# A GRU and an attention block on one core: q and k of a third head moved into the recurrent stage

## Time and profile before

| | |
|---|---|
| median of 3 runs | 793.98 us (793.65 to 794.06) |
| profiled execution | 792.58 us, its span 790.8 us |
| recurrent stage, 17 to 276 us | granted TensorE clock 0.88 |
| last products of the stage to steady attention, 276 to 296 us | clock 1.00, TensorE busy 15.9 of 20 us |
| attention, 296 to 700 us | TensorE busy 394.5 of 404 us |
| feed-forward, from 700 us | 90.8 us |

### The profile page before, as it was taken

How to read it: one execution, slowest core, us unless ns; L and a number is a source line. 1 busy time by engine, 2 the same in 40 slices (tenths; PEclk the granted TensorE clock), 3 DMA queues, 4 the chain that set the end, 5 groups by cost and what they waited for, 6 DMA issues and landing times.

```text
span 790.8 us, 25165 instructions
## 1 busy us (share of the span) xinstructions
PE 736.6 (93%) x10368; PEld 534.4 (68%) x10368; DVE 585.9 (74%) x1582; ACT 479.2 (61%) x1613; POOL 105.3 (13%) x131
## 2 busy tenths in 40 slices
PE   6899898898989889999999999999989999999997
PEld 5787777787777666666666666666666666644545
DVE  4777777777777777777788887788877888744553
ACT  4444555445454567666677666776668776666453
POOL 0222222222222110000020010020010200100030
PEclk8878989889899999999999999999999999999999
DMA  6121112111121012222222323222222222210001
GB/s 224 43 97 42 44 45 81 43 43 43 46 74 36 3 25 38 48 40 43 42 42 41 42 41 42 41 41 41 42 41 41 41 41 42 41 28 27 19 10 53
DMA packets 77465, 36.70 MB, mean 46 GB/s; under 512 B 70395, under 2 KB 73639, under 8 KB 77223
## 3 DMA queue, kind: packets, MB, share of 16 engines
q1 hardware_dynamic: 76775, 33.52, 19.2%
q10 hardware_dynamic: 576, 1.57, 0.5%
HBM read 16.20 MB, written 2.10 MB: 23 GB/s over the span
## 4 chain that ended last, share of the span: by engine, by line
PE 74%; DVE 11%; ACT 9%; issue 3%; DMA 2%; DVEq 0%; SPq 0%; POOL 0%; ACTq 0%; POOLq 0%
PE bank L394 18%; PE bank L395 17%; PE bank L396 17%; PE bank L495 11%; PE bank L502 5%; DVE h_hi L1113 3%; PE bank L414 3%; ACT prob L914 3%; ACT zg L856 2%; ACT nu L859 2%; DVE prob L1210 1%; DVE aT_lo L1225 1%; DVE mx L1193 1%; DVE p_lo L1204 1%; ACT p_hi L907 1%
## 5 line engine op out<-in xcount | busy, mean ns | idle before, releaser
L394 PE MATMUL bank<-y_hi,w_hi 128*128 128x512 f16 (+1 forms) x412 | 136.8, 338 | 0.2 <-DVE qk_lo L1089 0.2
L495 PE MATMUL bank<-h_hi,whh_hi 128*128 128x16 f16 x1536 | 111.1, 175 | 27.6 <-DVE h_hi L1113 26.6
L395 PE MATMUL bank<-y_hi,w_lo 128*128 128x512 f16 (+1 forms) x412 | 136.2, 337 | 0.0
L396 PE MATMUL bank<-y_lo,w_hi 128*128 128x512 f16 (+1 forms) x412 | 136.1, 337 | 0.0
L495 PEld LDWEIGHTS bank<-h_hi,whh_hi 128*128 128x128 f16 x1536 | 91.5, 98 | 51.0 <-DVE h_hi L1113 50.0
L914 ACT ACTIVATE prob<-bank,nmx 128x128 f32<-128x128 f32 x256 | 90.4, 365 | 35.2 <-DVE nmx L1196 35.2
L495 PE MATMUL bank<-h_hi,whh_lo 128*128 128x16 f16 x1536 | 108.5, 173 | 0.0
L495 PEld LDWEIGHTS bank<-h_hi,whh_lo 128*128 128x128 f16 x1536 | 91.6, 98 | 0.3 <-issue 0.3
L395 PE MATMUL bank<-w_hi,y_lo 128*128 128x128 f16 x512 | 89.1, 219 | 0.0
L396 PE MATMUL bank<-w_lo,y_hi 128*128 128x128 f16 x512 | 89.1, 219 | 0.0
L394 PE MATMUL bank<-w_hi,y_hi 128*128 128x128 f16 x512 | 89.1, 219 | 0.0
(11 more groups left out here) (157 smaller groups left out, 2171.3 us busy)
## 6 DMA issues: line engine op xcount, KB each, us to landing
stage<-in_weights SPq DMA_DIRECT2D x16, 640.0 KB, 3.9
x<-in_x SPq DMA_DIRECT2D x16, 128.0 KB, 3.9
out<-xr SPq DMA_DIRECT2D x3, 512.0 KB, 3.1
w<-in_ada_r SPq DMA_DIRECT2D x1, 1024.0 KB, 7.1
pT_hi<-p_hi SPq DMA_TRANSPOSE x64, 2.4
pT_lo<-p_lo SPq DMA_TRANSPOSE x64, 2.5
w<-in_W_ih ACTq DMA_DIRECT2D x2, 384.0 KB, 3.7
w<-in_W_hh ACTq DMA_DIRECT2D x2, 384.0 KB, 6.7
```

The lines of the kernel that those rows point to most:

```text
L394: mm(ps, w[0], a[0], start=start, stop=False, skip_group_check=True)
L395: mm(ps, w[1], a[0], start=False, stop=False, skip_group_check=True)
L396: return mm(ps, w[0], a[1], start=False, stop=stop, skip_group_check=True)
L495: nc.tensor.matmul(out(m0 + m), half[:, k, w], h_hi[:, k * B:(k + 1) * B, 1], start=False, stop=False, skip_group_check=True)
```

## The change

`AHEAD` becomes `(0, 8, 14)`. Fillers of 128 columns in a block become: step 0 twelve and two transposes, step 1 three and the biases, step 2 twelve, step 3 twelve, step 4 ten, step 5 twelve and two transposes, step 6 six, step 7 five (and the modulation). All three heads are now made two blocks behind. The last two blocks of tokens of heads 8 and 14 are made at d = 0, with 256 columns a product, each head in a bank of its own (7 and 4), and rounded at d = 1 and d = 2. `rows_sum` is one operation after step 7. The row modulation of block 0 starts a step later. In the attention steps of heads made ahead `values` comes before `project_out`. The gate of the out-projection signals each of its two halves. `hf` shares memory with `nat0`, and the program asks for a smaller scratch for DMA descriptors.

```diff
-AHEAD = (0, 14)
+AHEAD = (0, 8, 14)
-ITEMS = NA * NBL
+ITEMS = [(e, n, 1) for n in range(NBL - 2) for e in range(NA)] + [(0, NBL - 2, 1), (0, NBL - 1, 1)]
+ITEMS += [(e, NBL - 2, 2) for e in range(1, NA)]
-ROW_TILES = {1: (0, 0), 2: (0, 1), 4: (1, 0), 5: (1, 1)}
-ADA_AT = 3
+ROW_TILES = {2: (0, 0), 3: (0, 1), 4: (1, 0), 5: (1, 1)}
+ADA_AT = 1
+AHEAD_PLACE = {0: (0, (0, 1)), 2: (1, (0,)), 3: (1, (1,)), 5: (2, (0, 1))}
+AHEAD_HIGH = {0: 0, 3: 1, 5: 2}
+AHEAD_LOW = {0: (0, (0,)), 1: (0, (1,)), 4: (1, (0, 1)), 6: (2, (0, 1))}
...
+        def ahead_place(item, part):
+            e, n, blocks = ITEMS[item]
+            ps, width = bank[4 if n < NBL - 2 else (4, 7, 4)[e] if (e, n) != (0, NBL - 1) else 6], blocks * BS * B
+            at = slice((4 - 2 * blocks) * P + part * width, (4 - 2 * blocks) * P + (part + 1) * width)
+            return ps[:, at].rearrange("p (b t) -> p b t", b=B), slice(n * BS, (n + blocks) * BS)
...
-            tall_at = {1: (0, 3), 2: (3, 4), 3: (4, 5), 4: (5, 8), 5: (8, 9), 6: (9, 12)}
+            tall_at = (0, 0, 4, 5, 6, 9, 9, 12)
-            share = (0, 0, 3, 8, 14, 25, 29, 34, 36)
-            share_0 = (0, 0, 0, 2, 11, 15, 19, 27, 36)
+            share = (0, 0, 3, 9, 15, 25, 25, 31, 36)
+            share_0 = (0, 0, 0, 0, 6, 11, 16, 26, 36)
...
-                    if s == 0 and r > 1:
-                        ahead(0, r - 2, 1)
-                    elif s in (2, 3) and r > 1 and NA > 1:
-                        ahead(1, r - 2, s - 2)
-                    elif s == 7 and r > 0:
+                    if r > 1 and s in AHEAD_PLACE:
...
+                        e, parts = AHEAD_PLACE[s]
+                        ahead(NA * (r - 2) + e, parts)
+                    elif s == 7 and r == NBL - 1:
+                        ahead(NA * (NBL - 2))
...
                 for k in range(KD):
+                    if g > 0 and head == 0:
+                        pe.wait_ge(o_gated, KD * (g - 1) + k + 1)
...
                 if d > WHOLE[0] and i not in AHEAD:
                     keys(d)
+                if i in AHEAD:
+                    values(d)
                 if d >= LAG and not late:
                     project_out(d - LAG)
-                values(d)
+                if i not in AHEAD:
+                    values(d)
...
-                    for part in range(2 * NA - 2):
-                        ahead(1, NBL - 1, part)
+                    for e in range(1, NA):
+                        ahead(ITEMS.index((e, NBL - 2, 2)))
...
-                if d == 1 and NA > 1:
-                    ahead_high(1, NBL - 1)
+                if 0 < d < NA:
+                    ahead_high(ITEMS.index((d, NBL - 2, 2)))
...
-                    elif s == 6:
-                        rows_sum(r, slice(0, 6))
-                    elif s == 7:
-                        rows_sum(r, slice(6, BS))
+                    if s == 7:
+                        rows_sum(r)
```

More of the change, by code:

```diff
@@ L175, in build @@
         adar = w32[:, 0:KD * 4 * D].rearrange("p (k c) -> p k c", k=KD)
+        hf = nat0[:, :, :].rearrange("p (a j) d -> p a (j d)", a=2)
         bT = small[:, 0:NB]
@@ L468, in tall_parts, with ahead @@
                 return mm
[L470 to L482 removed]
+            def ahead(item, parts=(0, 1)):
+                e = ITEMS[item][0]
+                for part in parts:
+                    ps, t = ahead_place(item, part)
+                    if part == 0:
+                        pe.wait_ge(lb_lo, t.stop // BS)
+                        if item > 0:
+                            pe.wait_ge(qk_l, min(item, ITEMS.index((0, NBL - 2, 1)) + 1))
+                    w = SLOTS.index((part, AHEAD[e]))
+                    for k in range(KD):
+                        mm = product(ps, (wq_hi[:, w, k, :], wq_lo[:, w, k, :]), (y_hi[:, k, :, t], y_lo[:, k, :, t]),
+                                     k == 0, k == KD - 1)
+                    if part == 1:
+                        mm.then_inc(qk_mm, 1)
             tall_rest = [(k, i) for k in range(KD) for i in range(3)]
[L485 removed]
+            tall_at = (0, 0, 4, 5, 6, 9, 9, 12)
             def gru_step(r, s):
@@ L560, in _ @@
                             pe.wait_ge(lb_lo, NBL - 2)
-                        for i in range(*tall_at[s]):
+                        for i in range(tall_at[s], tall_at[s + 1]):
                             tall_parts(tall_rest[i % 6:i % 6 + 1], i // 6, early)
-                    elif G1 <= r - ADA_AT < ADA and s == 6:
+                    elif G1 <= r - ADA_AT < ADA and s == 7:
                         if r - ADA_AT == G1:
@@ L568, in _ @@
             rows_T(NBL - 1)
-            ahead(0, NBL - 2, 1)
             pe.wait_ge(lb_lo, NBL - 1)
@@ L573, in _ @@
             rows_back(NBL - 1)
-            for part in range(2 * NA - 2):
-                ahead(1, NBL - 2, part)
-            for part in range(2):
-                ahead(0, NBL - 1, part)
+            ahead(ITEMS.index((0, NBL - 1, 1)))
             def norm_rows(g):
@@ L1279, in _ @@
                 value_low(d)
-                if d == 1 and NA > 1:
-                    ahead_low(1, NBL - 1)
+                if 0 < d < NA:
+                    ahead_low(ITEMS.index((d, NBL - 2, 2)))
                 if d > 1:
```

99 lines of the change are left out of this document (37 added, 62 removed).

## The result

The changed kernel takes 788.85 us (median of 5 runs, 787.46 to 790.42) against 793.65 us for the kernel before (5 runs, 791.79 to 794.06): ratio 0.9939, 95% interval 0.9925 to 0.9953, 4.8 us faster. The forecast was 783.4 us with a range from 778.5 to 788.5; the direction was right, the gain less than half of it, and the time lies 0.35 us outside the range.

What follows compares the result with a forecast made beforehand. TensorE was taken to bound attention, the ScalarE and VectorE chain the recurrent steps. Terms - 6.0 - 1.7 - 0.3 - 3.0 - 0.6 + 1.0 = - 10.6 from 793.98 gave 783.4 us, range 778.5 to 788.5.

Steps and rivals of the forecast that it cites:

- the price of values first: Attention, heads 0 and 14: values ahead of out-projection remove 8.1 us of aT_lo waits, landings and scatter take part: 1.7 won.
- the clock's 3.0 us: Recurrent stage: more filler in light steps 5 to 1 leaves about two clock falls in place of ten: 3.0 us won.
- Head 8 leaves the attention: Attention: each group loses 12 products, 2.59 us; late landings take part back; 1.5 us a group, 6.0 for four.
- The sign of being wrong that was named: Attention, head 8: gaps of over 1.5 us before attend would show the forecast wrong.
- the two edits with the gates: Attention: 6.0 us from head 8, 1.7 from values before out-projection, 0.3 from the gate that signals by halves.
- The full gaps don't overrun: Recurrent steps 0 and 5: 0.95 of 1.06 us filled, cost 0 at full clock; rival of overrun had chance 0.10.
- Block 0: Start of recurrent stage: modulation a step later avoids waiting for the adaln bias: 0.6 us won, bounds 1.4 won, 0.5 lost.
- Between the stages: Recurrent stage to attention: longer last sum, wider products at d = 0 and subtractions cost 1.0 us, bounds 0.4 and 2.6.
- attention is held by softmax and DMA: Rival, attention: late landings leave head 8 0.7 us a group, values first nothing: 788.3 us, chance 0.14.
- with five falls: Middle case of the rival that the recurrent stage's clock falls as often as now (793.3 us, chance 0.08): 786 us.
- the bound: Recurrent stage, worst case of the clock term: 7 us lost, from ten falls at 1.1 us against 4.2.
- The sum: Whole kernel: - 6.0 - 1.7 - 0.3 - 3.0 - 0.6 + 1.0 = - 10.6 us, giving 783.4 us.

Runs made afterwards that it cites:

- busier: Changed kernel with 9 products of 128 columns per block, from block 2 on, made twice for nothing: 787.89 us, ratio 0.9913 to the kernel before.

## Why the prediction was wrong, point by point

Two terms of the sum failed: the price of values first, and the clock's 3.0 us. The other points are smaller.

**Head 8 leaves the attention: the mechanism was right, the size about so.** Forecast -6.0. Measured as the difference between the kernels without head 8 (394.0, 394.1 and 394.3 us) and those with it (387.6): -6.5. TensorE's work went down by 10.8 us by the table (48 products of 0.216 us are 10.4) and its idle time up by 4 to 5. This holds with the values first in both; with the out-projection first in both it is 389.6 against 393.5 us, -3.9, and then the other order brings -2.0. The sign of being wrong that was named, a gap of over 1.5 us before `attend` at head 8, showed in one group of four (1.75 us).

**Values first: this step failed.** It said that the values take more than each wait for `aT_lo`, "so these go", and priced the landing that comes in their place. It did not ask what the values wait for. They write the bank that VectorE reads for `v_lo` of the head before, and moved forward they come to it 0.4 us early. The changed kernel at d = 14 (VectorE, TensorE, SyncE's queue), to be held against the earlier trace rows:

```profile
365.45 0.68 DVE L1199 TENSOR_TENSOR v_lo<-bank,v_hi 128x512 f16<-128x512 f32 x1
...
365.79 0.22 PE L403 MATMUL bank<-kT_lo,qT_hi 128*128 128x128 f16 x1
366.19 0.23 PE L401 MATMUL bank<-w_hi,y_hi 128*128 128x128 f16 x1 [0.18 <-DVE v_lo L1199]
...
368.62 0.38 PE L403 MATMUL bank<-aT_lo,w_hi 128*128 128x512 f16 x1
369.20 0.23 PE L401 MATMUL bank<-pT_hi,v_hi 128*128 128x128 f16 x1 [0.20 <-DMA pT_lo<-p_lo]
...
366.70 1.22 SPq L294 DMA_TRANSPOSE pT_lo<-p_lo  x1
```

That is 366.19 - 365.79 - 0.06 = 0.34 us here and at head 8, 0.6 us at head 0, and 4.6 us over eleven such heads. The waits for landings were priced at 11 x 1.1 = 12 us and are 8.6. Forecast for the two edits with the gates: -8.0; measured -5.9. The edit by itself, on the kernel before, gave nothing. The gate by halves was not undone alone; what it is worth stays open.

**The clock in the recurrent stage: the term of 3.0 us was mis-sized.** The direction was right: from 7 to 9 falls in blocks 2 to 13 to between 1 and 4, 2.9 in the mean. For these blocks I had 4.2 us lost before and 1.4 after, 2.8 won; measured against the same twelve blocks of 16.12 us it is 3.7 lost before and 3.2 after, 0.5 won. Of the 2.3 us that are missing:

- 0.5: the one profile lost 4.2, the mean of three is 3.7.
- 0.8: 2.9 falls at 0.75 us are 2.2 and not 1.4.
- 0.6: even a block without a fall takes 16.17 us and not 16.12. Step 1 is 2.02 us long, because VectorE waits in step 0 for ScalarE's rounding; with the sum of rows in two operations it is 1.98 again, so the six more products and the later sum make it together. The forecast had 0 here.
- 0.35: in block 13 VectorE stands still for 0.46 us before one `h_hi`, in all three profiles of the kernel before (step 4) and all nine of the changed code (step 3). I had counted it among the falls. Its cause the profiles don't show.

Blocks 14 and 15 gave 0.8 where I had 0.2: none of the nine has a fall there.

A fall before cost (197.1 - 193.4 - 0.35)/8 = 0.4 us, one now costs 0.75, though the clock was mostly low for 6.8 us then and for 3.4 us now. Two things differ. A fall now meets step 6 behind the twelve products of step 5. And the forecast took the block's one step of 2.25 us as fixed, which it is not: it is the step whose `h_hi` scan takes 0.56 us in place of 0.29, and in the kernel before it is missing in most blocks with a fall (it is there in 4, 6 and 7 of twelve blocks of the three profiles, in all twelve of the changed kernel). So a fall there came with 0.27 us less in the same block. In the first profile of each kernel ScalarE's rounding of a weight (`w_hi`) and GpSimd's `xb_lo` run beside each such scan; which of them makes it long was not tried, and 12 x 0.27 = 3.2 us lie there in the changed kernel. The clock of 0.95 was right and said little of the time: low clock is dear only where the gap is full.

**The full gaps don't overrun.** Steps behind twelve fillers are 1.98 us long, and with three products more still 2.00 (busier). So the row's 0.056 us per product was the price, and not the 81 ns that the Trainium skill gives for such a stream (TensorE: Matmul & The Clock Gate, Back-to-back issue gap): by that, fifteen products would take 1.2 us, an estimate from that page, in a gap of 1.06.

**Block 0: not measurable.** The stretch to block 2 scatters from 46.5 to 48.3 us over all profiles, and that hides the 0.6 us.

**Between the stages: +1.7 instead of +1.0.** The one profile before was the mild one of three. My term left the clock out: in all eleven profiles of this layout the clock fell there, so that the products from 279.55 on are 0.107 us apart where they had been 0.056. It fell in two of three profiles of the kernel before too, and in one of four with the gap filled. The fillers of block 14 that left are the likely reason, but the longest wait there grew only from 1.52 to 1.85 us (before 277.84), so that they are the reason is argued and not shown.

**The rival that came nearest** was "attention is held by softmax and DMA", at 788.3 us, to which I gave 0.14. Its place was right: taking the low half's landing away brings 6.0 us. Its reason, that head 8 itself wouldn't pay, was wrong, and that its time lies 0.6 us from the measured one is luck: it needs the 3.0 us of the recurrent stage, which were not there. A slip among the rivals: with five falls at the 1.1 us that the bound takes for each, the sum gives 787.5 and not 786 us.

**The sum.** Forecast -10.6 and measured, by stretches, -5.3: of the 5.3 us that are missing attention has 2.1, the blocks 1.7, block 0 0.8 and the gap 0.7. By the medians it is 4.8 us won, and 5.8 are missing.

## What to carry to other kernels

When an instruction is moved forward on its engine, list what it waits for at the new place: the reader of the buffer that it overwrites counts as much as its operands. Where a transfer lands late, look at its issue before you add buffers: here one of twice the size was worth 3 us of attention and second buffers 1. And measure a stretch in several executions before pricing a term of one or two us by it; kernels that share its code are free samples.

## What the runs showed of the hardware

- An issue of a transpose on SyncE's queue takes 1.2 us for 512 or 1024 columns; landings follow the issue by 2.45 and 3.07 us at the median. In the changed kernel 31 of 128 land more than 3.0 us behind it, at most 4.8. In 11 of these the issue itself takes over 2 us (up to 2.5); in 8 of the 11 the high half of the same head is still in flight when it starts, in 3 no other transfer of the program, and what makes it so is open. The Trainium skill (DMA: Bandwidth & Descriptors, Anatomy of one DMA) gives a fixed cost of some 2.0 us beside the one by size, for another kind of queue; here 2.45 - 0.62 = 1.8 us is what the size doesn't explain.
- A second queue for the low half, which would test the same thing, was not tried: the Trainium skill (Advanced Engine Details and Errata, X-Bar Transpose (TRN2)) allows one stream of transposes at a time. No run here shows it.
- In blocks 2 to 13 of the changed kernel nearly every fall of the clock to 1.2 GHz lasted 3.4 us, and falls in blocks that follow each other came 17.06 us apart. A loop whose period with a fall is 17.03 us took one in each of twelve passes; one of 16.17 us (16.92 with a fall) mostly for two or three passes in a row. With other products in the block two falls a pass came, 6.8 and 10.2 us apart. Nine useless products per block made the kernel no slower (787.89 against 788.85 us, intervals overlapping).
- An addition of 0.50 us on VectorE in step 6 did no harm in the kernel before; with the two subtractions of the third head beside it (0.60 us for both) step 7 grew from 1.98 to 2.19 us.
- The same scan on VectorE takes 0.29 us, and 0.56 us at one place in a block, with a rounding on ScalarE and a subtraction on GpSimd beside it.
